# GNN + mixture-of-experts layer: where GpSimd and ScalarE split x into its high and low part

## The reference

```python
def gnn(h, ...):                       # h = layernorm(x), 2500 edges
    m = relu(concat(h[src], edge_attr) @ W1.T + b1) @ W2.T + b2
    agg = segment_sum(m, dst)
    gi = agg @ W_ih.T + b_ih           # 3*512 columns: r, z, n
    gh = h @ W_hh.T + b_hh
    r = sigmoid(i_r + h_r);  z = sigmoid(i_z + h_z)
    n = tanh(i_n + r * h_n)
    h_new = (1 - z) * n + z * h
    return h + gamma * (h_new - run_mean) * rsqrt(run_var + eps) + beta

x = x + gnn(layernorm(x), ...)
x = x + ffn(layernorm(x), ...)         # gate: top 2 of 8 experts (512 -> 32 -> 512), and a shared one
```

## Time and profile before

| What | Before |
|---|---|
| median of 3 runs | 1365.17 us |
| the profiled execution, its time and its span | 1365.4 us, 1363.6 us |
| TensorE matmul busy | 1318.7 us, 97% |
| VectorE (DVE) busy | 945.4 us, 69% |
| GpSimd (POOL) busy | 830.0 us, 61% |
| ScalarE (ACT) busy | 762.6 us, 56% |

### The profile page before, as it was taken

The page is one execution under the profiler, slowest core; times in us unless marked ns, Lnnn a source line. Parts: engine busy times, 40 slices in busy tenths (PEclk is TensorE's granted clock), DMA queues, the critical chain, the costliest instruction groups (busy, mean ns, idle before and its releaser), DMA issues. The chain is left out here.

```text
span 1363.6 us, 22871 instructions
## 1 busy us (share of the span) xinstructions
PE 1318.7 (97%) x6420; PEld 1095.8 (80%) x6420; DVE 945.4 (69%) x2117; ACT 762.6 (56%) x1744; POOL 830.0 (61%) x1121
## 2 busy tenths in 40 slices
PE   6999999999879999999999999999999999999995
PEld 4778888888668888888888888888888888888884
DVE  5576434234377787777777787778777877787775
ACT  4521323212466666667666666666666676666652
POOL 4211142103477777777777777777777777777771
PEclk9999999999989999999999999999999999999998
DMA  8223544246433433334343433343434333343330
GB/s 321 74 78 114 165 148 143 93 156 244 182 101 118 138 126 128 120 133 135 119 130 124 138 119 134 117 138 123 131 117 137 125 129 119 135 133 121 125 107 31
DMA packets 62864, 179.58 MB, mean 132 GB/s; under 512 B 9328, under 2 KB 9968, under 8 KB 62704
## 3 DMA queue, kind: packets, MB, share of 16 engines
q1 hardware_dynamic: 46912, 99.20, 21.4%
q0 software_dynamic: 15920, 79.97, 17.5%
HBM read 141.86 MB, written 37.29 MB: 131 GB/s over the span
## 5 line engine op out<-in xcount | busy, mean ns | idle before, releaser
L1609 PE MATMUL bank<-whh_hi,x_hi 128*128 128x512 f32 x948 | 377.7, 398 | 11.7 <-DVE x L1555 10.6
L1609 PE MATMUL bank<-whh_hi,x_lo 128*128 128x512 f32 x948 | 370.0, 390 | 0.0
L1609 PE MATMUL bank<-whh_lo,x_hi 128*128 128x512 f32 x948 | 370.0, 390 | 0.0
L1609 PEld LDWEIGHTS bank<-whh_hi,x_hi 128*128 128x128 f32 x948 | 178.5, 188 | 48.1 <-DVE x L1555 11.0
L1609 PEld LDWEIGHTS bank<-whh_hi,x_lo 128*128 128x128 f32 x948 | 178.2, 188 | 38.4
L1609 PEld LDWEIGHTS bank<-whh_lo,x_hi 128*128 128x128 f32 x948 | 178.7, 189 | 34.5
L1355 POOL TENSOR_TENSOR rstd<-var_eps,minus_half 128x1 f32<-128x1 f32 x158 | 90.2, 571 | 149.1 <-DVE var_eps L484 149.1
L509 ACT ACTIVATE h<-xt,shift,rstd 128x512 f32<-128x512 f32 x79 | 64.5, 816 | 113.0 <-POOL one_rstd L1361 113.0
L1346 POOL DMA_INDIRECT gates<-gates_in,slot_at x79 | 84.9, 1075 | 60.4 <-issue 46.4
L1400 POOL TENSOR_TENSOR n_pre<-r_hn,gates 128x512 f32<-128x512 f32 x79 | 102.9, 1303 | 13.3 <-POOL r_hn L1396 13.2
L1547 DVE TENSOR_TENSOR bank<-bank,h_n 128x512 f32<-128x512 f32 x79 | 55.3, 700 | 71.4 <-POOL h_n L1408 71.4
(11 more groups left out here) (186 smaller groups left out, 3077.1 us busy)
## 6 DMA issues: line engine op xcount, KB each, us to landing
xt<-in_x SPq DMA_DIRECT2D x79, 256.0 KB, 2.9
x_lo_raw<-in_x_cols SPq DMA_DIRECT2D x79, 256.0 KB, 2.7
out<-y SPq DMA_DIRECT2D x79, 256.0 KB, 2.0
gates_in<-g_out SPq DMA_DIRECT2D x16, 768.0 KB, 3.9
wih_lo_raw<-in_wih_t SPq DMA_DIRECT2D x4, 768.0 KB, 15.1
whh_rows<-in_whh SPq DMA_DIRECT2D x4, 768.0 KB
whh_lo_raw<-in_whh_t SPq DMA_DIRECT2D x4, 768.0 KB, 7.7
gates_in<-late_out SPq DMA_DIRECT2D x6, 256.0 KB, 7.1
```

What stands on the lines that cost most here:

```text
L1609: last = pe.matmul(to[0:R, :], a[:, s, k * R:(k + 1) * R], w[:, k, q * D:(q + 1) * D], start=n == 0, stop=n == 3 * DK - 1)
```

## The change

In GpSimd's period `x_low` moves from its place between `n_pre` and `h_n` to the front, ahead of the second norm's factor. In ScalarE's period `x_high` moves from behind `first_rows` to the front. No operation is added or removed, and no semaphore is changed.

```diff
@@ GpSimd, body(p) @@
+                if p.has(1) and not p.early(1):
+                    x_low(pool, p)
                 if p.has(-1):
                     norm(p, -1, 2)
...
                     pool.tensor_tensor(n_pre[:, :], r_hn[:, :], gates[:, s, 2 * D:G3], ALU.add).then_inc(n_pre_done, 1)
-                if p.has(1) and not p.early(1):
-                    x_low(pool, p)
                 if p.has(0):
                     s = p.slot(0)
                     pool.wait_ge(n_done, t + 1)
@@ ScalarE, body(p) @@
+                if p.has(1) and not p.early(1):
+                    x_high(act, p)
                 if p.has(1) and not p.first(1):
                     first_rows(act, p)
-                if p.has(1) and not p.early(1):
-                    x_high(act, p)
```

## The result

| | Before | After |
|---|---|---|
| median of 4 runs each, on one chip | 1365.11 us (1364.88 to 1365.42) | 1355.98 us (1355.57 to 1356.38) |
| the profiled execution, its time and its span | 1365.4 us, 1363.6 us | 1355.6 us, 1353.7 us |

The ratio is 0.9933, 95% interval 0.9921 to 0.9945: the changed kernel is 9.1 us faster. The prediction said 4.6 and a range that ended at 1359.6. The direction and the main mechanism hold; the size is off by a factor of two.

The account below looks back on a forecast made before the run. The prediction took a closed loop of waits through GpSimd and DVE as the bound, just above TensorE's 12.28 us. Gains 4.2 + 0.14 + 0.29 = 4.6 gave 1360.6 us; likeliest case 1359.8 to 1361.6, 8 in 10 within 1359.6 to 1364.2.

Parts of the forecast that it names:

- The ring: Node stage: closed loop of waits through GpSimd and DVE, ScalarE beside it, TensorE not in it; 12.37 us, bounds the stage.
- the ring becomes 12.37 - 0.48 = 11.89 (11.85 from the mean of 12.33): GpSimd, `n_pre` to `h_n`: without `x_lo` the loop of waits shortens by 0.48 of its 1.26 us.
- the one thing that is in the ring: GpSimd: the second norm's factors, queued behind the moved `x_lo`, were taken to be part of the loop of waits.
- `x_lo` hidden at the front of the period: GpSimd after the gather: `x_lo`'s 1.26 us fits the 1.81 idle before `var_eps`, leaving 0.55; room for lateness 0.98.
- The rival of a hidden tail of the gather: GpSimd: the gather runs up to 1.81 us past its row, `x_lo` starts late, kernel slower; chance 0.08, SBUF clash included.
- No clash in SBUF: `x_lo` beside DVE's L1549 to L1557: no stretch taken; bound from above 0.93 us, under the 0.98 of room.
- `x_hi` and the lead of `h2`: ScalarE: `x_hi`'s 0.52 us fits 1.41 idle ahead of `h`; `h2` then ends 0.6 to 0.9 before its transposes.
- TensorE's own pace: z gate, transposes to next transposes: a period with nothing late takes 12.05 + 0.23 = 12.28 us.
- 76 x 12.28 = 933.3: Steady node-stage periods at TensorE's pace: 933.3 instead of 937.1 us, gain 3.8, or 4.6 with 12.27; taken as 4.2.
- Start and end: Edges of the node stage: L1547 earlier by about 0.14 us at the second tile and about 0.29 at the end.
- The rival "nothing is gained": Node stage: TensorE, busy 100%, is bound by something else, 1365.2 us; nothing or at most half gained, chance 0.22.

Follow-up runs that it names:

- e10: The kernel before with one 128x1 copy added on GpSimd right behind `x_h_b`: 1373.63 us, ratio 1.0058.
- e9: The kernel before with the transposes of `h2` behind three instead of six matmuls of the z gate: 1367.32 us, ratio 1.0013.
- e12: The changed kernel with four 128x1 copies added on GpSimd right behind `x_h_b`: 1365.41 us, ratio 0.9999 against the kernel before.
- e5: The kernel before with one 128x1 copy added on GpSimd behind the second norm's factors: 1365.38 us, ratio 0.9998.
- e7: The changed kernel with three 128x1 copies added on GpSimd behind the second norm's factors: 1355.76 us, ratio 0.9930 against the kernel before.
- e1: The changed kernel with `x_high` back behind `first_rows` on ScalarE, so GpSimd's half alone: 1356.52 us, ratio 0.9933 against the kernel before.
- e2: The kernel before with only ScalarE's half of the change, `x_hi` at the front of its period: 1365.66 us, ratio 0.9999.
- e3: The kernel before with `x_lo` taken off GpSimd and made on DVE behind `hid_lo`: 1356.37 us, ratio 0.9930.
- e6: The changed kernel with one 128x1 copy added on GpSimd behind the second norm's factors: 1356.25 us, ratio 0.9931 against the kernel before.
- e11: The changed kernel with two 128x1 copies added on GpSimd right behind `x_h_b`: 1356.77 us, ratio 0.9933 against the kernel before.
- e13: The changed kernel with one 128x1 sigmoid into scratch on ScalarE ahead of its early idle time: 1355.23 us, ratio 0.9924 against the kernel before.

## Why the prediction was right, and where it was wrong

**The ring.** Right in what sets the period of the kernel before (e10 adds 0.107 to the ring and gets 0.104 a period; e9 moves TensorE's work and gets nothing), and in its length: for the step "the ring becomes 12.37 - 0.48 = 11.89 (11.85 from the mean of 12.33)" e12 gives about 11.85 and 0.47 for the 0.48. Wrong in its course. The prediction calls the second norm's factors "the one thing that is in the ring"; e5 and e7 show them beside it, and the ring goes from DVE's L1573 through ScalarE's L1435 to GpSimd's L1382. It changed no term of the sum. It made e5 miss and, with the 0.42 that three copies take instead of 0.45, e7.

**`x_lo` hidden at the front of the period.** Right. It starts where the gather ends, takes 1.30 and leaves `rstd` a wait of 0.67. The rival of a hidden tail of the gather is refuted by the 0.03 between its row and the start of `x_lo`.

**No clash in SBUF.** Right. `x_lo` takes 1.30 beside DVE's L1551 to L1557, which take 0.69 to 0.70 as elsewhere; over the kernel, `x_lo` has a mean of 1308 ns after and 1299 before. By the rule of the Trainium skill that the prediction cites (page SBUF — State Buffer, section "Who interferes with whom") the stretch is 0, and the trace agrees.

**`x_hi` and the lead of `h2`.** `x_hi` fits as said, but is not needed (e1, e2). `h2` came 1.05 ahead instead of 0.6 to 0.9. Against the transposes L1547 has moved from 821.89 - 815.66 = 6.23 to 816.76 - 811.56 = 5.20, so by 1.03 instead of 0.85: it starts 0.08 behind the start of L1541 and not behind its end, and L1541 itself lies 0.06 nearer to the transposes. This changes no time.

**TensorE's own pace: the failed step.** The prediction says "A period in which nothing is late is therefore 12.05 + 0.23 = 12.28 us". It is 12.21 in the profiled execution and 12.22 in six others. The 0.23 of the plain gap was right (0.232 measured). The 12.05 was taken as TensorE's undisturbed work from one pair of transposes to the next, while `h2` was late in that very period too. Its first step holds the transposes' weight loads, which could not start ahead of time because their operand was not there, and it was 0.06 longer for it. Measured, the stretch is 12.046 before and 11.988 in the six other kernels whose `h2` is early (e1, e3, e6, e7, e11, e13), and that first step fell from 0.411 to 0.353: the difference of 0.058 is all in it. In the profiled execution of the changed kernel the stretch is 11.973, another 0.015 shorter: a third of its periods are 12.18, where all those of the six between 480 and 1320 us are 12.22. The Trainium skill, page TensorE: Matmul & The Clock Gate, section "Step-by-step: what each phase is for", states that TensorE pulls a weight load ahead of matmuls in flight if the row groups don't conflict or the load goes to the background weight buffer. As to the pulling ahead, the trace after agrees, with the loads 0.23 ahead, and before they could not be pulled; no run here shows the two conditions. The term "76 x 12.28 = 933.3" should have been 927.6, and its gain 9.46 instead of 4.2 (928.7 and 8.3 by the six others). The row that would have told it was there: 22.1 us of waits of the weight loads for `h2`, 0.32 in each period, in the view of waits. That is idle time of the loads and not the price, which is 0.05 ahead of the transposes and 0.06 inside them. The prediction looked for late starts among the matmuls alone.

**Start and end.** The start gave 0.08 for 0.14 predicted, the end 0.47 for 0.29. Small terms, and of the right size.

**The rival "nothing is gained"** rested on TensorE busy 100% of the stage. It is as busy by this view after the change, in periods 0.12 us shorter: a row of 0.39 covers a start that comes 0.31 behind the one ahead of it. The view can't show that a TensorE bound is real.

## What to carry to other kernels

Where an engine loses a little at one place in every period, find the undisturbed pace from a stretch in which the operand is truly early, and look at the weight loads beside the matmuls: here a late operand that is loaded as weights cost ahead of the matmul and again inside it. Work that stands inside a closed ring of waits between engines is worth moving even by a single small instruction, and where it goes matters little as long as there is a wait of the same size. To measure a ring's slack, add short instructions at a place in it that no wait follows, until the time moves. A copy that vanishes in a wait tells that this place is beside the ring, and the row of that wait names the engine through which the ring goes.

## What the runs showed of the hardware

- Four 128x128 weight loads that start 0.23 ahead of their matmuls leave 0.35 from the transposes to the next matmul (after); started together with them they leave 0.41 (before).
- A copy of one column on GpSimd, 0.18 in its row, takes the engine for 0.11 in the mean (e10), and four in a row take 0.47 (e12).
- The same subtraction of 128x512 takes 0.68 on DVE (e3) and 1.30 on GpSimd.
- Not explained: in the profiled execution of the changed kernel a third of the periods take 12.18 and the mean is 12.206, while six other kernels with the gain have 12.22 throughout (means of 12.220 and 12.221). It makes 1.1 us over the 76 periods, about as much as the spread of the runs' times.
